# Inverse roots of both layer norms as a power on GpSimd, with new stage lists for the attention loop

## The reference

```
h = emb[x] + (lora_A[:, x]).T @ lora_B.T * 2
z = layernorm(h);  qkv = z @ Wqkv + bqkv          # 16 heads of 16
local  = softmax(q k / 4, |i - j| <= 64) v        # a band
globl  = softmax(q k[:64] / 4) v[:64]             # the first 64 keys
gate   = sigmoid(z @ Wg + bg)
h = h + ((1 - gate) * local + gate * globl) @ Wout + bout
x2 = layernorm(h)                                 # (h - mean) / sqrt(var + 1e-5)
h = h + x2 + moe(x2)                              # 8 experts, top 2 by softmax(x2 @ router), capacity
```

## Time and profile before

| what | us |
|---|---|
| median of 3 runs (lowest, highest) | 3839.25 (3838.16, 3849.77) |
| the profiled execution, its own time | 3837.03 |
| its span, first to last instruction | 3834.7 |
| set-up, up to about | 60 |
| attention loop, up to about | 2260 |
| expert stage | the rest |

### The profile page before, as it was taken

How to read it: one execution, slowest core, us unless ns; L and a number is a source line. 1 busy time by engine, 2 the same in 40 slices (tenths; PEclk the granted TensorE clock), 3 DMA queues, 4 the chain that set the end, 5 groups by cost and what they waited for, 6 DMA issues and landing times. The chain is left out here.

```text
span 3834.7 us, 117863 instructions
## 1 busy us (share of the span) xinstructions
PE 3447.8 (90%) x47729; PEld 2806.7 (73%) x47729; DVE 2241.1 (58%) x5390; ACT 1988.1 (52%) x3118; POOL 2337.5 (61%) x2663
## 2 busy tenths in 40 slices
PE   2889898889899898888889739999999999999998
PEld 1565565656565555566565539999999999999998
DVE  3577777777867777777777534443444444343343
ACT  0566665666666666656666524444444444444443
POOL 5467777777777777777776644444444455444443
PEclk7899999999999999999999869999999999999999
DMA  4444444444444544444544223232323333222222
GB/s 138 146 143 154 129 146 144 131 148 137 148 134 146 139 147 134 145 146 130 152 135 148 66 86 59 52 66 49 72 48 70 58 60 74 45 51 45 46 45 41
DMA packets 242539, 398.30 MB, mean 104 GB/s; under 512 B 34572, under 2 KB 150748, under 8 KB 242044
## 3 DMA queue, kind: packets, MB, share of 16 engines
q1 hardware_dynamic: 168540, 297.43, 24.9%
q0 software_dynamic: 70512, 91.16, 13.5%
q10 hardware_dynamic: 3008, 2.95, 0.2%
HBM read 198.55 MB, written 192.88 MB: 102 GB/s over the span
## 5 line engine op out<-in xcount | busy, mean ns | idle before, releaser
L1351 POOL DMA_INDIRECT out_y<-out_t,tok_out x264 | 424.9, 1609 | 732.6 <-DMA out_y<-out_t,tok_out 397.9
L1497 ACT ACTIVATE act<-psS 128x512 f32<-128x512 f32 x528 | 316.0, 599 | 870.7 <-PE psS L1425 870.7
L1559 DVE TENSOR_TENSOR h_lo<-act,h_hi 128x512 fp32r<-128x512 f32 x528 | 367.4, 696 | 553.0 <-ACT h_hi L1498 553.0
L879 ACT ACTIVATE pl<-psS 128x896 f32<-128x896 f32 x512 | 468.4, 915 | 281.2 <-PE psS L727 275.5
L1460 PE MATMUL psO<-w_hi,h_hi 128*128 128x256 f32 x2112 | 598.5, 283 | 0.0
L1460 PE MATMUL psO<-w_lo,h_hi 128*128 128x256 f32 x2112 | 588.7, 279 | 0.0
L1460 PE MATMUL psO<-w_hi,h_lo 128*128 128x256 f32 x2112 | 587.6, 278 | 0.0
L556 POOL TENSOR_SCALAR_AFFINE_SELECT pl<-pl 128x512 f32<-128x512 f32 x512 | 354.8, 693 | 361.8 <-ACT pl L879 360.8
L1425 PE MATMUL psS<-xg_hi,w_hi 128*128 128x256 f32 x1984 | 551.6, 278 | 0.0
L1425 PE MATMUL psS<-xg_hi,w_lo 128*128 128x256 f32 x1984 | 551.3, 278 | 0.0
L1425 PE MATMUL psS<-xg_lo,w_hi 128*128 128x256 f32 x1984 | 551.2, 278 | 0.0
(11 more groups left out here) (229 smaller groups left out, 7741.8 us busy)
## 6 DMA issues: line engine op xcount, KB each, us to landing
qk_scr<-qk SPq DMA_DIRECT2D x64, 768.0 KB, 4.0
Q<-qk_scr SPq DMA_DIRECT2D x128, 384.0 KB, 4.7
K<-qk_scr SPq DMA_DIRECT2D x128, 384.0 KB, 5.5
qk_scr<-qk SPq DMA_DIRECT2D x64, 512.0 KB, 3.4
qk_scr<-qk SPq DMA_DIRECT2D x64, 256.0 KB, 3.5
h_rows<-held SPq DMA_DIRECT2D x32, 512.0 KB
hb<-h_rows SPq DMA_DIRECT2D x32, 512.0 KB
out_y<-h SPq DMA_DIRECT2D x32, 512.0 KB
```

The costliest lines, as they stand in the source:

```text
L879: act.activation(pl[:, v, half, :, lo:hi], psS[:, 0:2, lo:hi], ACT.Exp, scale=SCALE).then_inc(exp_done, 1)
L1351: pool.indirect_dma_start(out=y[:, :], in_=out_t[:, tile.out, s, :], in_offset=None, out_offset=bass.IndirectOffsetOnAxis(ap=tok_out[:, ti ...
L1497: act.activation(act32[:, b, :, 0:cols], src, ACT.Silu)
L1559: dve.tensor_tensor(h_lo[:, 2 * b:2 * b + 2, 0:cols], act32[:, b, :, 0:cols], h_hi[:, 2 * b:2 * b + 2, 0:cols].bitcast(F32), ALU.subtract) ...
```

## The change

The two square roots on ACT are gone, with their constant `eps_b`. DVE adds eps to the variance (stages `var1`, `var2`, 128x4), and POOL raises the sum to the power of minus one half by a `tensor_tensor` with the ALU operation `pow` and a constant tile of -0.5 (stages `rstd1`, `rstd2`, 128x4). DVE's reciprocals are gone. All five lists are new: apart from these stages each holds the same stages as before, in another order, and the passes are cut at another place. Of each list the lines are shown here that hold the stages of the change and those near them, the list of TensorE in its new form in full.

```diff
-        eps_b = keep("eps_b", [P, 1])
+        neg_half = keep("neg_half", [P, QB])
...
-                    dve.memset(eps_b[:, :], EPS)
+                    dve.memset(neg_half[:, :], -0.5)
...
             ORDER["pe"] = (
...
-                ("nxt", "qk", 2), ("nxt", "qk", 3), ("cur", "exp", 1), ("cur", "max", 14), ("prev", "mix", 0), ("cur", "exp", 2),
-                ("cur", "max", 15), ("cur", "exp", 3), ("prev", "mix", 1), ("cur", "max", 16), ("cur", "exp", 4), ("cur", "out", 0),
-                ("cur", "max", 17), ("prev", "mix", 2), ("cur", "exp", 5), ("cur", "out", 1), ("cur", "exp", 6), ("cur", "max", 18),
-                ("cur", "m_rows", 2), ("cur", "exp", 7), ("cur", "max", 19), ("prev", "mix", 3), ("cur", "out", 2), ("cur", "exp", 8),
...
-                ("cur", "exp", 14), ("cur", "out", 6), ("cur", "out", 7), ("nxt", "max", 5), ("cur", "exp", 15), ("nxt", "m_rows", 0),
...
+                ("cur", "max", 19), ("cur", "out", 3), ("past", "ahead", None), ("cur", "exp", 8), ("prev", "attn_t", 0),
+                ("nxt", "max", 0), ("cur", "exp", 9), ("cur", "m_rows", 3), ("prev", "attn_t", 1), ("nxt", "max", 1),
+                ("far", "embed", None), ("prev", "project", 0), ("nxt", "max", 2), ("cur", "exp", 10), ("prev", "project", 1),
+                ("cur", "exp", 11), ("nxt", "max", 3), ("far", "lora", 0), ("cur", "out", 4), ("cur", "exp", 12), ("nxt", "max", 4),
+                ("cur", "out", 5), ("cur", "exp", 13), ("far", "lora", 1), ("nxt", "max", 5), ("cur", "exp", 14), ("cur", "out", 6),
+                ("cur", "out", 7), ("cur", "exp", 15), ("nxt", "max", 6), ("cur", "out", 8), ("cur", "exp", 16), ("nxt", "max", 7),
+                ("prev", "x2_t", 0), ("nxt", "m_rows", 0), ("cur", "exp", 17), ("nxt", "max", 8), ("prev", "x2_t", 1),
+                ("nxt", "values", 0), ("nxt", "max", 9), ("cur", "out", 9), ("cur", "exp", 18), ("prev", "router", None),
+                ("nxt", "values", 1), ("cur", "exp", 19), ("nxt", "max", 10), ("cur", "out", 10), ("nxt", "m_rows", 1),
+                ("cur", "out", 11), ("nxt", "values", 2), ("nxt", "max", 11), ("far", "xn_t", 0), ("far", "xn_t", 1),
+                ("nxt", "exp", 0), ("nxt", "max", 12), ("far", "qk", 0), ("nxt", "exp", 1), ("far", "qk", 1), ("far", "qk", 2),
+                ("nxt", "max", 13), ("far", "qk", 3), ("nxt", "max", 14), ("nxt", "exp", 2), ("cur", "mix", 0), ("nxt", "exp", 3),
+                ("nxt", "max", 15), ("nxt", "out", 0), ("nxt", "exp", 4), ("nxt", "max", 16), ("cur", "mix", 1), ("nxt", "max", 17),
+                ("nxt", "exp", 5), ("nxt", "out", 1), ("nxt", "m_rows", 2), ("cur", "mix", 2), ("nxt", "exp", 6), ("nxt", "out", 2),
+                ("nxt", "max", 18), ("cur", "mix", 3), ("nxt", "exp", 7),
             )
             ORDER["act"] = (
...
-                ("cur", "exp", 11), ("cur", "exp", 12), ("prev", "std2", None), ("cur", "exp", 13), ("cur", "evac", (1, 1)),
...
-                ("far", "std1", None), ("cur", "exp", 19), ("nxt", "values", 0), ("nxt", "values", 1), ("nxt", "m_rows", 1),
...
+                ("cur", "exp", 13), ("cur", "exp", 14), ("cur", "evac", (1, 1)), ("cur", "exp", 15), ("cur", "exp", 16),
...
+                ("nxt", "evac", (0, 0)), ("nxt", "exp", 7), ("prev", "weights", None), ("nxt", "exp", 8), ("cur", "attn_t", 0),
...
             )
             ORDER["dve"] = (
-                ("nxt", "rstd1", None), ("cur", "cut", (1, 0)), ("cur", "kg", 1), ("cur", "cut", (1, 1)), ("old", "rank", 3),
...
-                ("cur", "gate2", None), ("past", "top", 6), ("prev", "mix", (2, 2)), ("past", "top", 7), ("cur", "max", 18),
-                ("past", "top", 8), ("cur", "max", 19), ("prev", "mix", (3, 0)), ("cur", "cut", (3, 0)), ("cur", "cut", (3, 1)),
...
-                ("far", "lora", 0), ("nxt", "max", 3), ("prev", "rstd2", None), ("prev", "scale2", 0), ("nxt", "kg", 0),
...
+                ("past", "top", 5), ("cur", "max", 12), ("nxt", "qk", 0), ("past", "top", 6), ("nxt", "qk", 1), ("cur", "max", 13),
+                ("nxt", "qk", 2), ("past", "top", 7), ("nxt", "qk", 3), ("cur", "max", 14), ("prev", "mix", (0, 0)),
...
+                ("prev", "mix", (1, 1)), ("prev", "mix", (1, 2)), ("past", "top", 8), ("cur", "max", 17), ("prev", "mix", (2, 0)),
...
+                ("prev", "stats2", 0), ("nxt", "max", 4), ("prev", "stats2", 1), ("nxt", "cut", (0, 0)), ("prev", "var2", None),
...
+                ("prev", "scale2", 1), ("prev", "scale2", 2), ("nxt", "max", 6), ("prev", "scale2", 3), ("past", "rank", 2),
...
+                ("far", "stats1", 1), ("far", "var1", None), ("nxt", "max", 9), ("nxt", "cut", (1, 0)), ("nxt", "gate1", None),
+                ("nxt", "cut", (1, 1)), ("nxt", "cut", (1, 2)), ("far", "scale1", 0), ("past", "rank", 4), ("far", "scale1", 1),
...
             )
             ORDER["pool"] = (
...
-                ("next", "gather", 2), ("old", "scatter", 5), ("old", "scatter", 6), ("old", "scatter", 7), ("cur", "sel", 15),
...
-                ("nxt", "sel", 3), ("next", "gather", 4), ("cur", "mix", 0), ("cur", "mix", 1), ("next", "gather", 5), ("nxt", "sel", 5),
...
+                ("cur", "sel", 6), ("prev", "mix", 2), ("prev", "mix", 3), ("far", "gather", 7), ("old", "scatter", 4),
+                ("old", "scatter", 5), ("old", "scatter", 6), ("cur", "sel", 7), ("cur", "sel", 8), ("cur", "sel", 10),
...
+                ("prev", "rstd2", None), ("old", "scatter", 7), ("cur", "sel", 15), ("cur", "sel", 16), ("cur", "sel", 17),
+                ("next", "gather", 0), ("prev", "residual", 0), ("far", "rstd1", None), ("cur", "sel", 18), ("next", "gather", 1),
...
+                ("cur", "mix", 0), ("cur", "mix", 1), ("next", "gather", 5), ("next", "gather", 6), ("nxt", "sel", 5),
             )
             ORDER["sp"] = (
...
-                ("nxt", "m_in", 1), ("far", "qk_write", (0, 0)), ("far", "qk_write", (0, 1)), ("far", "qk_write", (0, 2)),
...
+                ("past", "y", None), ("nxt", "qk_write", (1, 0)), ("nxt", "qk_write", (1, 1)), ("nxt", "qk_write", (1, 2)),
+                ("prev", "hb", None), ("nxt", "load", 0), ("cur", "m_out", 2), ("cur", "m_in", 2), ("cur", "m_out", 3),
+                ("nxt", "load", 1), ("cur", "m_in", 3), ("nxt", "load", 2), ("prev", "x2", None), ("nxt", "m_out", 0),
+                ("nxt", "m_in", 0), ("nxt", "load", 3), ("nxt", "m_out", 1), ("far", "hold", None), ("far", "qk_write", (0, 0)),
+                ("far", "qk_write", (0, 1)), ("nxt", "m_in", 1), ("far", "qk_write", (0, 2)),
             )
...
+                        if stage == "rstd1":
+                            pool.wait_ge(var1_done, s + 1)
+                            pool.tensor_tensor(rstd1[:, :], var1[:, :], neg_half[:, :], ALU.pow).then_inc(rstd1_done, 1)
+                        if stage == "rstd2":
+                            pool.wait_ge(var2_done, s + 1)
+                            pool.tensor_tensor(rstd2[:, :], var2[:, :], neg_half[:, :], ALU.pow).then_inc(rstd2_done, 1)
...
-                        if stage == "std2":
-                            act.wait_ge(mv2_done, s + 1)
-                            act.activation(std2[:, :], mv2[:, :, 1], ACT.Sqrt, bias=eps_b[:, :]).then_inc(std2_done, 1)
-                        if stage == "std1":
-                            act.wait_ge(mv1_done, s + 1)
-                            act.activation(std1[:, :], mv1[:, :, 1], ACT.Sqrt, bias=eps_b[:, :]).then_inc(std1_done, 1)
...
-                        if stage == "rstd2":
-                            dve.wait_ge(std2_done, s + 1)
-                            dve.reciprocal(rstd2[:, :], std2[:, :]).then_inc(rstd2_done, 1)
+                        if stage == "var2":
+                            dve.wait_ge(mv2_done, s + 1)
+                            dve.tensor_scalar(var2[:, :], mv2[:, :, 1], EPS, None, ALU.add).then_inc(var2_done, 1)
...
-                        if stage == "rstd1":
-                            dve.wait_ge(std1_done, s + 1)
-                            dve.reciprocal(rstd1[:, :], std1[:, :]).then_inc(rstd1_done, 1)
+                        if stage == "var1":
+                            dve.wait_ge(mv1_done, s + 1)
+                            dve.tensor_scalar(var1[:, :], mv1[:, :, 1], EPS, None, ALU.add).then_inc(var1_done, 1)
```

More of the change, by code:

```diff
@@ L364, in build @@
             mv1 = tmp("mv1", [P, QB, 2])
-            std1 = tmp("std1", [P, QB])
+            var1 = tmp("var1", [P, QB])
             rstd1 = tmp("rstd1", [P, QB])
@@ L395, in build @@
             mv2 = tmp("mv2", [P, QB, 2])
-            std2 = tmp("std2", [P, QB])
+            var2 = tmp("var2", [P, QB])
             rstd2 = tmp("rstd2", [P, QB])
@@ L473, in build @@
-                ("cur", "exp", 17), ("nxt", "max", 8), ("prev", "router", None), ("cur", "exp", 18), ("nxt", "values", 0),
-                ("nxt", "max", 9), ("cur", "exp", 19), ("nxt", "values", 1), ("cur", "out", 9), ("nxt", "max", 10), ("cur", "out", 10),
```

(20 more changed lines are left out.)

57 lines of the change are left out of this document (19 added, 38 removed).

## The result

The changed kernel takes 3695.17 us (median of 4 runs, 3690.48 to 3699.59), the kernel before 3844.51 us beside it (3838.16 to 3853.59): ratio 0.961, interval 0.9583 to 0.9636, 149 us faster. The forecast was 3740 us in a range of 3670 to 3845, a gain of 102. The sign held, and the three waits that the forecast wanted gone are gone; the size was a third too low.

A forecast was written before the change was run, and what follows sets the result against it. TensorE was taken as the bound, with idling and slow clock to win in the attention loop. Terms 2.35 + 1.1 + 1.05 - 1.2 = 3.3 us a pass, times 30, plus 3, gave 3740 us, range 3670 to 3845.

The forecast's parts named there:

- L734's stall for ACT: Scores of the global keys: PE's 1.71 us wait a pass goes with rstd2's root and table loads; 2.35 with clock.
- local scores for ACT: Score tiles on PE: of 1.09 us a pass waiting for ACT, the new list removes 0.8; 1.1 with clock.
- L707's stall for DVE: Maxima tile, max 19 behind a held DVE addition: 1.54 us a pass, taken at half, 1.05 with clock.
- new waits, less small ones gone: Charge of 1.2 us a pass, clock included, for new waits in untraced lists, covering the power's upper end.
- clock: Attention loop: each us of PE idling charged 0.38 us more for the slow clock, from 2.6 / 6.9.
- rival B: DVE's small two-input operations held by POOL elsewhere: one place 3772 us, chance 0.20; two 3837, sharing 0.08 with waits only moving.
- The power: POOL's power on 128x4 taken at 0.5 us, bounds 0.18 to 1.16; cover at rstd2 0.55 us, so no cost.
- rival A: Slow power makes rstd2 and max 6 late; gain gone at 2.9 us; chance 0.12, including a late load or wait.
- xn_t comes much later: rstd1 has four small DVE steps between var1 and scale1, with xn_t much later: its power costs nothing.
- ACT: Losing two roots and four table loads, 5.7 of 41.0 us a pass, leaves ACT near 35 us a pass.
- Rival C: Waits only move, DVE and POOL balance holds the pass: 3825 to 3850 us; chance 0.08, shared with two DVE holds.
- Loads of K: Loads take 5.5 us to land, each released by the same score tile; reordered DMA issue costs nothing.

The follow-up runs named there:

- old_top_late: Kernel before, with only the small additions top 7 and top 8 on DVE moved behind max 19: 3781.34 us, ratio 0.9835.
- old_power_both: Kernel before with power on POOL ahead of sel 12, scale2 0 behind lora 1, top 7 and 8 behind max 19: 3782.32 us, ratio 0.9853.
- changed_again: The changed kernel unaltered, measured again beside the third group's kernels: 3699.23 us, ratio 0.9639 of the kernel before.
- three_powers2: Changed kernel with the power of rstd2 computed three times, the first two to a spare tile: 3815.08 us, ratio 0.9952; ratio 0.9941 in another group.
- scale1_early: Changed kernel with the last scale1 on DVE moved ahead of the router stages: 3731.87 us, ratio 0.9704 of the kernel before.
- old_lists_power: Kernel before with the power on POOL, its old lists changed only in the exchanged stages: 3906.56 us, ratio 1.0163.
- coef_psum_early: Changed kernel with the last scale1 early and the sum's reciprocal left in PSUM for coef: ratio 0.9731 of the kernel before.

## Why the prediction was right, and where its size was off

The sum, in us of idling a pass and without the clock, step by step:

| term | predicted | measured | where seen |
|---|---|---|---|
| L734's stall for ACT | 1.71 | 1.7 | 43.7 us down to 1.7 |
| local scores for ACT | 0.8 | 1.1 | 27.9 down to 0.7 |
| L707's stall for DVE | 0.77 | 1.5 | gone from the list |
| new waits, less small ones gone | -0.87 | -0.7 | 4.3 gone, idling down by 3.65; L845's alone is 0.9 |
| idling | 2.4 | 3.65 | |
| clock | 0.9 | 0.96 | busy 59.0 to 58.0 |
| a pass | 3.3 | 4.6 | |

**The stall at L734**: right in place and size. It stays in old_top_late (41.3 us) and in the new lists with the root, and goes in every kernel without it (4.1 us in all at most). What the forecast didn't see is that the removal alone is no gain: in the old lists it comes out at 1.016, as DVE then waits for the power and the held addition costs PE 2.4 us a pass in place of 1.54. In the old lists with both repaired, old_power_both, the 1.71 are still not in the time: it is level with old_top_late. Of the combinations tried only the new lists turn them into time.

**The stall at L707** is the mis-sized term: taken at half, for fear that the held addition would turn up elsewhere; it went whole, and that is 0.77 of the 1.25 us of idling by which the sum fell short. old_top_late shows that it is that addition, and that moving it alone is worth 63 us, 2.1 a pass. That this is the upper value of the prediction is luck in its parts: 0.7 us of idling and 1.4 of busy time, not 1.54 and 0.6. In the changed kernel the hold did turn up elsewhere, up to 3.20 us long, and PE feels it where it does: in 4 of 25 passes it waits 2.0 us at L811 for the `qk_rest` behind it, 8.0 us in all, 0.3 a pass (7 passes and 14.1 us in changed_again). So rival B was right in what happens on DVE, and its price came at a fifth.

**The local scores**: 0.8 taken of 1.09, and all went. The wait is there in every kernel with the old TensorE list (24.7 to 37.4 us) and in none with the new one by more than 1 us in all.

**The power**: 1.04 to 1.12 us where 0.5 was taken, near the upper bound. The cover was larger than the 0.55 worked out: DVE waits for `rstd2` only 0.2 us a pass (4.4 us in 25), so some 0.85 us are covered. It is used up, as three_powers2 shows, and then a us costs 1.9 in all, 1.0 of it idling by the chain that rival A named. By an estimate from its 0.5% at 3.1 us, the gain would be gone a little above that length. But `rstd1`, which was given nothing, is what shows: DVE idles 15.0 us for it in 25 passes, and PE waits 23.3 us for `xn`, the largest wait that is left. The step that failed is "xn_t comes much later": it does, but the held fourth `scale1` stands in between, at 1.40 us in 18 of 22 passes, where it takes 0.40 in scale1_early. There the wait is gone, and other holds cost more.

**The clock** came out right in amount, 0.96 us where 0.9 was forecast, but by luck. Before, the time at half clock was 130 us of the 1680 (5.1 a pass), as the prediction has it, and PE idles in only 5 of them; after, it is 1.0 us a pass. Half of the difference would be 2.0 us. Only 0.96 are seen, so the same matmuls are busy some 1 us a pass longer at full clock than before, and no run shows why. Nor does the clock follow the sum of idling, as the factor of 0.38 a us assumes:

| kernel | PE idle, us a pass | clock | wait at max 19, us a pass |
|---|---|---|---|
| old_lists_power | 7.3 | 0.93 | 2.4 |
| before | 6.9 | 0.96 | 1.54 |
| old_top_late | 6.2 | 0.99 | none |
| old_power_both | 6.4 | 1.00 | none |

It goes with the stall at max 19. In the trace of before, 85 of the 130 us follow that stall (18 of the 22 instances over 1 us have a slow stretch behind them), and 34 follow L734's (10 of 25). Half of that is 1.7 and 0.7 us a pass. So one factor for every us of idling was right for L734's stall, to which it gives 0.65, and far too low for the other.

**ACT** went to 853.45 / 24.6 = 34.7 us a pass, as forecast (near 35). The drain that the Trainium skill (ScalarE: Activation LUTs, What ACT_TABLE_LOAD costs) adds to each switch would, by an estimate from its figure, have brought it to about 30; the trace disagrees again. No table load is left in the loop. **Rival C**, that waits only move, fails for the changed kernel, but is what old_power_both shows in the old lists beside old_top_late. Loads of K, which the forecast held to be in time, are: PE waits for them 2.7 us in all.

The remaining 8 us, between 141 of the profiled executions and 149 of the medians, are the spread of the runs: the profiled execution of before, 3837.03 us, is below all four of its runs.

## What to carry to other kernels

On an engine that isn't the bound, read who is queued behind a wait before removing the work that causes it: the same removal came with a kernel 1.6% slower or 1.1% faster, as its consumer stood two places earlier or later in the list, and with 3.9% faster only with all lists laid out anew. A small DVE operation with both inputs in SBUF, placed beside a run of POOL work, can cost twenty times its time (3.77 us for 0.19); look for it by the maximum of its duration, not the median, and place it where PE has other work, or give it a PSUM input. When a stall is removed by a move, count which passes still meet it at its new place, and split what the run shows into idling and busy time before calling a price confirmed: 63 us came as expected here, in other parts than expected.

## What the hardware showed that was not expected

**A power on POOL costs by the instruction or by the column far more than a subtraction.** 1.04 us for 128x4, against 0.18 for a copy of that size and 1.16 for a subtraction of 128x512. Which of the two isn't tried.

**DVE held by POOL.** The hold isn't for one POOL instruction: `coef` began at 945.02, and POOL's instructions ended at about 946.97, 947.56, 948.14 and 948.73 before `coef` ended at 948.79. Reductions on DVE were not held: `negm`, L968, takes at most 0.83 us in all of the changed kernel, but reads PSUM; of those that read SBUF, `m_cut`, L983, takes at most 0.19 us and `zgate`, L1182, 1.22 us in all 32. Held were the additions and products with two SBUF inputs, but also copies and scalings with one, as `xn`, L1172, at 1.41 us. The Trainium skill (SBUF — State Buffer, Who interferes with whom) says that a DVE instruction with two SBUF inputs contends with a GpSimd instruction that reads SBUF, that copies and scalings can, and that reductions never do. The trace agrees in all three, and with coef_psum_early in the remedy. The page has the one that comes later wait for the whole instruction of the other; here it waited over several. What decides when it is let go wasn't settled.

**The clock and the stall.** The granted clock of the steady loop was 0.96 with the stall at max 19, 0.93 where that stall was longer, and 0.99 where it alone was taken away, with the sum of PE's idling between 6.2 and 7.3 us a pass in all three. In the changed kernel each of the four 2.0 us waits at L811 has a stretch at half clock behind it, 13.7 us in all, over half of what the loop has left.
